# Layer-norm statistics of the last chunk in one pass, squares on ScalarE

## The reference

```python
x = x + _L0_attn_ref(_layernorm(x, axis=-1), Wq, Wk, Wv, Wp)   # attn_ref returns x + out @ Wp
x = x + _L0_ffn_ref(_layernorm(x, axis=-1), weight, aux_weight1, aux_weight2, bias)
# layernorm: m = mean(x), v = var(x), (x - m) / sqrt(v + 1e-5), over the 1024 features
# ffn_ref:   tanh(x @ weight @ aux_weight1 @ aux_weight2 + bias)
```

## Time and profile before

| | us |
|---|---|
| runs | 1335.19, 1416.9 (median 1376.05) |
| the profiled execution, its own time | 1336.31 |
| its span, from first to last instruction of the slowest core | 1334.4 |
| spans of the 8 cores | 1323.1 to 1334.4 |
| busy: PE, DVE, ACT, POOL | 1004.9, 419.6, 718.2, 66.8 |

### The profile page before, as it was taken

One profiled execution on the slowest core, in us unless ns is written; L12 is line 12 of the kernel. 1 busy time (PEld: TensorE's weight loads), 2 busy tenths in 40 slices (PEclk: granted clock), 3 DMA queues, 4 the chain that ended last, 5 costly groups with the idle time before them and its releaser, 6 DMA issues.

```text
span 1334.3 us, 15366 instructions; the slowest of 8 cores (1323.1 to 1334.4 us)
## 1 busy us (share of the span) xinstructions
PE 1004.9 (75%) x5185; PEld 334.0 (25%) x5185; DVE 419.6 (31%) x558; ACT 718.2 (54%) x678; POOL 66.8 (5%) x80
## 2 busy tenths in 40 slices
PE   2255999885677777788997878898777879877376
PEld 1011444441122222222222222232222223222022
DVE  3695000446601101234222223422222342222454
ACT  0122222005589897497677649767754976774002
POOL 2000000000000000000110000011000001202000
PEclk9766999995599999999998999999899999988579
DMA  9900000131000000501543350164334015877601
GB/s 232 176 2 0 0 1 1 16 33 16 0 1 0 1 1 1 63 1 15 66 56 64 56 63 1 17 64 57 63 60 58 1 17 64 102 112 101 81 1 63
DMA packets 85113, 57.65 MB, mean 43 GB/s; under 512 B 2088, under 2 KB 79920, under 8 KB 84016
## 3 DMA queue, kind: packets, MB, share of 16 engines
q0 software_dynamic: 79040, 39.85, 26.2%
q1 hardware_dynamic: 6000, 16.82, 3.7%
HBM read 88.12 MB, written 8.39 MB: 72 GB/s over the span
## 4 chain that ended last, share of the span: by engine, by line
PE 43%; ACT 16%; DVE 7%; issue 6%; DMA 2%; DVEq 0%; ACTq 0%; POOLq 0%
ACT S L714 14%; PE sc L524 9%; PE pvs L726 9%; PE dns L736 6%; PE lnps L633 4%; PE wps L633 4%; PE wps L546 2%; PE lnps L651 2%; DMA wbuf<-wp 2%; PE lnps L546 2%; PE wps L651 1%; DVE S L749 1%; DVE S L747 1%; PE lnps L577 1%; DVE S L614 1%
## 5 line engine op out<-in xcount | busy, mean ns | idle before, releaser
L714 ACT ACTIVATE S<-sc,cbias 128x1024 bf16<-128x1024 f32 x512 | 550.2, 1110 | 190.0 <-PE dns L739 176.5
L524 PE MATMUL sc<-qb,kb 64*128 64x512 bf16 x512 | 200.5, 392 | 117.0 <-ACT S L714 107.6
L726 PE MATMUL pvs<-S,vt 128*64 128x512 bf16 x512 | 212.9, 416 | 26.5 <-DVE S L749 26.5
L731 PE MATMUL pvs<-S,vt 128*64 128x512 bf16 x512 | 213.7, 417 | 0.0
L528 PE MATMUL sc<-qb,kb 64*128 64x512 bf16 x512 | 204.5, 400 | 0.0
L739 PE MATMUL dns<-S,ones 128*64 128x512 bf16 x512 | 203.0, 396 | 0.0
L736 PE MATMUL dns<-S,ones 128*64 128x512 bf16 x512 | 202.8, 396 | 0.0
L524 PEld LDWEIGHTS sc<-qb,kb 64*128 64x128 bf16 x512 | 47.5, 93 | 341.6 <-issue 341.6
L327 PE MATMUL pj<-S,vt 128*128 128x512 bf16 x448 | 99.3, 385 | 6.3 <-ACT qb L294 3.9
L726 PEld LDWEIGHTS pvs<-S,vt 128*64 128x64 bf16 x512 | 54.9, 107 | 149.4 <-issue 149.3
L747 DVE COPY S<-pvs 128x512 f32<-128x512 f32 x32 | 22.1, 691 | 190.3 <-PE dns L739 168.3
(11 more groups left out here) (144 smaller groups left out, 1114.2 us busy)
## 6 DMA issues: line engine op xcount, KB each, us to landing
wbuf<-w POOLq DMA_DIRECT2D x36, 512.0 KB, 7.7
xr<-x SPq DMA_DIRECT2D x4, 2048.0 KB, 24.2
out<-xr SPq DMA_DIRECT2D x32, 256.0 KB, 2.2
wbuf<-wp POOLq DMA_DIRECT2D x14, 512.0 KB, 7.9
vt<-w POOLq DMA_DIRECT2D x8, 512.0 KB, 22.4
vt<-wq POOLq DMA_DIRECT2D x4, 512.0 KB, 31.9
vt<-wk POOLq DMA_DIRECT2D x4, 512.0 KB, 49.3
wbuf<-wv POOLq DMA_DIRECT2D x4, 512.0 KB, 32.3
```

What stands on the lines that cost most here:

```text
L524: TE.matmul(scs[sl][:, 0:512], kb[0:64, 2048 * p + 128 * m: 2048 * p + 128 * (m + 1)], qb[0:64, 2048 * p + 512 * c: 2048 * p + 512 * (c + 1)],
L714: ins = SE.activation(p_un[sl], scs[sl][:], AF.Exp, bias=cbias[:], scale=0.125)
L726: TE.matmul(pvs[0:64, :], vt[:, 1024 * m + 128 * p: 1024 * m + 128 * p + 64], p_un[sl][:, 0:512], start=(m == 0), stop=(m == NM - 1), tile ...
L731: TE.matmul(pvs[64:128, :], vt[:, 1024 * m + 128 * p + 64: 1024 * m + 128 * (p + 1)], p_un[sl][:, 512:1024], start=(m == 0), stop=(m == NM ...
```

## The change

For the last chunk (`flush=True`) the two passes are replaced by one. `emit_stats1_j` casts block j once, alternating between two buffers; the sum's matmul (into lnps) follows; ACT squares the cast into one of two further buffers, and a second matmul sums it into dns. `emit_stats1_fin` computes mean and variance from both accumulators. The buffers lie in vtmp, where mean and rstd are written only after the last matmul. For the other chunks `emit_stats_j` stays, but for the two waits on the output DMAs, which are gone for all chunks.

```diff
--- before.py
+++ after.py
@@ -496,6 +496,8 @@
                 "wp_ev": 0,
                 "wps_free": (s_ve, 0),
                 "xbf_free": 0,
+                "sq_done": [0, 0],
+                "sq_mm": [0, 0],
                 "mean_ev": 0,
                 "var_ev": 0,
                 "rstd": 0,
@@ -563,8 +565,6 @@
                     VE.wait_ge(s_te.h, st["xbf_free"])
                 if j == 0 and which == 0:
                     VE.wait_ge(s_ve.h, st["wp_ev"])
-                    VE.wait_ge(d_o[0].h, d_o[0].n)
-                    VE.wait_ge(d_o[1].h, d_o[1].n)
                 mcast = s_ve.inc(VE.tensor_copy(xbf, xr_j[:, j, 512 * cw:512 * (cw + 1)]))
                 src = xbf
                 if which == 1:
@@ -577,6 +577,47 @@
                 ins = TE.matmul(acc[:], ones128[:], src,
                                 start=(j == 0), stop=(j == NCH - 1))
                 st["xbf_free"] = s_te.inc(ins)
+
+            def emit_stats1_j(cw, j):
+                sl = j % 2
+                xb = [vtmp[:, 0:512], vtmp[:, 512:1024]][sl]
+                xq = [vtmp[:, 1024:1536], vtmp[:, 1536:2048]][sl]
+                if j == 0:
+                    while wp_q:
+                        wp_q.pop(0)()
+                    VE.wait_ge(s_ve.h, st["wp_ev"])
+                if st["sq_mm"][sl]:
+                    VE.wait_ge(s_te.h, st["sq_mm"][sl])
+                if st["sq_done"][sl]:
+                    VE.wait_ge(s_se.h, st["sq_done"][sl])
+                mcast = s_ve.inc(VE.tensor_copy(xb, xr_j[:, j, 512 * cw:512 * (cw + 1)]))
+                TE.wait_ge(s_ve.h, mcast)
+                if j == 0:
+                    wait_mark(TE, acc_free[1])
+                    wait_mark(TE, acc_free[3])
+                ins = TE.matmul(accs[1][:], ones128[:], xb,
+                                start=(j == 0), stop=(j == NCH - 1))
+                s_te.inc(ins)
+                SE.wait_ge(s_ve.h, mcast)
+                st["sq_done"][sl] = s_se.inc(SE.activation(xq, xb, AF.Square,
+                                                           bias=0.0, scale=1.0))
+                TE.wait_ge(s_se.h, st["sq_done"][sl])
+                ins = TE.matmul(accs[3][:], ones128[:], xq,
+                                start=(j == 0), stop=(j == NCH - 1))
+                st["sq_mm"][sl] = s_te.inc(ins)
+                st["xbf_free"] = st["sq_mm"][sl]
+
+            def emit_stats1_fin(cw):
+                VE.wait_ge(s_te.h, st["xbf_free"])
+                st["mean_ev"] = s_ve.inc(VE.tensor_scalar(mean_c, lnps[:], 1.0 / D,
+                                                          None, ALU.mult))
+                VE.wait_ge(s_ve.h, st["mean_ev"])
+                m1 = s_ve.inc(VE.tensor_mul(rstd_c, mean_c, mean_c))
+                VE.wait_ge(s_ve.h, m1)
+                st["var_ev"] = s_ve.inc(VE.scalar_tensor_tensor(
+                    rstd_c, accs[3][:], 1.0 / D, rstd_c, ALU.mult, ALU.subtract))
+                acc_free[1] = (s_ve, st["var_ev"])
+                acc_free[3] = (s_ve, st["var_ev"])
 
             def emit_stats_fin(cw, which):
                 VE.wait_ge(s_te.h, st["xbf_free"])
@@ -674,10 +715,15 @@
 
             def tail_thunks(cw, flush=False):
                 th = []
-                for which in range(2):
+                if flush:
                     for j in range(NCH):
-                        th.append(lambda w=which, j=j: emit_stats_j(cw, w, j))
-                    th.append(lambda w=which: emit_stats_fin(cw, w))
+                        th.append(lambda j=j: emit_stats1_j(cw, j))
+                    th.append(lambda: emit_stats1_fin(cw))
+                else:
+                    for which in range(2):
+                        for j in range(NCH):
+                            th.append(lambda w=which, j=j: emit_stats_j(cw, w, j))
+                        th.append(lambda w=which: emit_stats_fin(cw, w))
                 th.append(lambda: emit_rstd(cw))
                 for jp in ((0, 1), (2, 3), (4, 5), (6, 7)):
                     th.append(lambda jp=jp: emit_apply(cw, list(jp)))
```

## The result

The changed kernel takes 1319.17 us (median of 7 runs, 1315.54 to 1319.79) against 1337.06 us before (median of 6). One of the six, of 1416.9 us, fell in a slower state that programs on all 8 cores show now and then, with a lower granted clock on the cores of one die, and the ratios here leave such runs out. The ratio is 0.9868, with a 95% interval of 0.9851 to 0.9884. That is 15.5 to 19.9 us less, 17.6 in the middle; 15.5 were forecast, and 1320.8 us for the time. The change is 1.3%, and its interval is clear of no change. The profiled execution took 1316.56 us.

A forecast was written before the change was run, and what follows sets the result against it. The last chunk's statistics were taken as pure latency: 26.77 us becomes 11.4, plus 0.14 from the removed waits, a gain of 15.5 us. From the profiled 1336.3 us that gave 1320.8 us, range 1314 to 1329.

The forecast's parts named there:

- What bounds the stage: Last chunk's statistics, 26.77 us: no engine full, nothing beside it, pure latency; every us saved comes off the end.
- The round: One-pass statistics with two buffers: one cast-to-cast round covers two blocks in 2.05 us, 1.03 per block.
- The square's price: ACT square of 128x512 in the statistics: 0.63 us, with 0.48 and 0.72 as ends.
- The sum of the stage: First cast to end of variance: three rounds 6.15, odd block's lag 0.86, last block 1.87, finish 2.29; total 11.4 us.
- a clock that rises within the stage: Statistics matmuls of 0.38 instead of 0.58 us: at most 0.8 us off, 1320.0 us, counted within the forecast case.
- The tail of the odd block: In each round of the statistics, PE's program order makes the odd block trail the even one by 0.86 us.
- The waits on the output DMAs: Two waits removed before the first cast: 0.14 us gained there, nothing beyond, since the transfers landed long before.
- Behind the stage: Applies and projections after the statistics: nothing shifts in kind; applies stay DVE-bound, first group at 1.2 GHz paid again.
- Table loads: Rival: Square in the statistics needs another activation table, two loads, 2.6 us; gain 12.9, 1323.4 us; chance 0.05.
- No overlap: Rival: each statistics block cast only after the previous is summed, stage 18.7 us; gain 8.2, 1328.1 us; chance 0.08.
- The clock comes back and lasts: Rival: clock rises in the statistics and lasts through the applies, together about 2.2 us, 1317.8 us; chance 0.05.
- Slower through the clock: Rival: high clock does not return in the dense projections, 22 groups slow, 37 us in all, 1358 us; chance 0.02.

The follow-up runs named there:

- the five kernels above: Kernel before without output-DMA waits (1.0011); changed kernel with those waits put back (0.9899), square on DVE (0.9881), one buffer (0.9941), or added matmuls in the applies (0.9847).
- the kernel with added matmuls: Changed kernel with three unused matmuls behind each of the first projection's first seven matmuls, during the applies; ratio 0.9847.

## Why the prediction was right

**What bounds the stage.** Right: it was latency with no other work beside it, and the 16.0 us that left it are not found again behind it.

**The round.** Right: 2.05 us forecast, 2.06 measured at the low clock, 1.84 where the clock was high for part of the round, and 2.05 for each block with one buffer. The square's price was 0.63 us, 0.627 measured.

**The sum of the stage.** 11.4 us forecast, 10.66 measured, and nearly all of the difference is the clock. The three rounds took 1241.40 - 1235.66 = 5.74 us instead of 6.15, since only the middle one had slow matmuls throughout; the last block's way to the end of its sum of squares took 1.67 instead of 1.87, since its last matmul took 0.38 us and not 0.58. That is 0.6 us. The finish started 0.11 us behind that sum instead of 0.18, which is 0.07 more and not the clock's. The prediction had put a price of up to 0.8 us on a clock that rises within the stage and left it in the forecast's range without adding it: that was the term that was too small. It had also taken the clock as low from the start, while the stage began at 1.00, left from the residual groups, and lost it only within the slice from 1237.

**The tail of the odd block.** 0.86 us forecast from PE's order, as two slow matmuls; 1242.26 - 1241.40 = 0.86 measured. In part this is luck. The reason holds where the matmuls are slow (1238.33 - 1237.50 = 0.83). In the last round they are fast, two of them would take 0.43, and the odd block's sum of squares waits for its square (1241.71, "<-ACT") and not for the matmul ahead of it: the lag of the slow round was carried on, as each buffer closes a loop of its own.

**The waits on the output DMAs.** Right: 0.13 us, shown by their removal alone.

**Behind the stage.** Costed at nothing; it gave 0.4 us (68.98 to 68.56 in the mean of the eight cores, and the same way on each). The clock was back 3.6 us behind the start of the applies' last matmul (1260.87 to about 1264.5), and before 4.5 us behind it (1279.96 to 1284.5); why it came back sooner is not shown. So the parts that can be read from the traces are 16.0 + 0.13 + 0.4 = 16.5 us, and with a tenth from the residual groups they are the 16.6 us of the whole tail, inside the measured 15.5 to 19.9. Of these 16.6 us the forecast had 15.5; the clock within the stage (0.6) and what came off behind it (0.4) are most of the rest, and both had been put at nothing in the sum. What the median shows beyond 16.6 lies ahead of the tail, where the stage's start on the median core was 1233.9 us before, 1230.0 in the changed kernel, and between 1230.0 and 1231.7 in the five kernels above that keep the residual groups as they were, the kernel before without its waits (1231.5) included, which gained nothing. I take it for the spread between executions; its cause is open and was not looked for.

**The rivals.** Table loads: none. No overlap: it is the kernel with one buffer, which had been put at 18.7 us for the stage (18.44 measured); two buffers did overlap. The clock comes back and lasts: it did come back (0.68 in the slice from 1240, then 1.00) and did not last; the kernel with added matmuls shows that its price was right (2.2 us). Slower through the clock: the dense groups were back at 1.73 us within the first projection.

## What to carry to other kernels

In a stage where each engine is busy about half the time or less and nothing runs beside it, count the handovers in the loop that a buffer closes: one more buffer was worth about as much here (7.8 us) as a whole pass left out (8.2 us), and covering the stage with the matmuls ahead of it another 4.2. Which engine does an operation mattered less than which buffers made it wait. And put an independent instruction between one that writes and one that reads on DVE: its operations of 0.69 us then start 0.60 us apart and not 0.80.

## What was not expected of the hardware

- DVE starts an operation before the one ahead has ended, if it doesn't wait for it: 0.34 us behind one of 0.43, 0.60 behind one of 0.69. Where it waits for the one directly ahead, and reads what that wrote, it is 0.52 and 0.80. Waiting for a neighbour thus costs 0.2 us, which over the fifteen steps between the sixteen operations of the applies was 2.9 us. Whether it is the wait or the dependency, no run here separates.
- When the square was on DVE, the clock was not lost while the matmuls of the statistics ran, on any core. The sixteen came 0.43 us apart on the mean, the first 0.8 us behind the first cast; in the changed kernel, which lost it, they came 0.46 us apart, the first 0.94 us behind. On five cores, the slowest among them, the granted clock was 1.00 up to the end of the variance, and on three it fell some 1.5 us before that, behind the last matmul. What made the difference to the changed kernel is not shown. Three slices of the slowest core:

```profile
1236.00:1238.00 2.00, 0.39 (x2) 0.19 (x2) 1.76 (x4) 0.00 (x0) 0.00 (x0) 1.00 1.27 153
1238.00:1240.00 2.00, 1.69 (x5) 0.41 (x5) 1.69 (x6) 0.00 (x0) 0.00 (x0) 1.00 1.21 145
1240.00:1242.00 2.00, 1.69 (x6) 0.45 (x5) 1.79 (x5) 0.00 (x0) 0.00 (x0) 1.00 1.43 187
```

- How long the first dense work stays slow is not the same for the same instructions: from the variance to the end it took 69.0, 68.5, 68.9 and 67.7 us in four kernels that are alike there (before, changed, square on DVE, one buffer), and with one buffer 69.3 and 69.4 on two cores of the same execution. In slices of 1 us, counted from the end of the variance, the high clock was back in the 20th, 19th, 19th and 18th, and on those two cores in the 21st. What sets the instant is not shown. A difference of up to 1.6 us between kernels can be of this kind.
